# A graph layer on one core: adjacency moved against stationary features, instead of features moved against stationary adjacency

## The reference

```
h = maximum(layernorm(x), 0)
deg = sum(adj, axis=1) + 1e-5
out = (adj / deg) @ h @ W_neigh.T + b_neigh + h @ W_self.T + b_self
result = x + relu(out)
```

## Time and profile before

| | |
|---|---|
| median of three runs | 439.43 us |
| profiled execution, span from first to last instruction | 437.5 us (no other time is given for it) |
| TensorE busy | 423.0 us |
| VectorE busy | 210.6 us |
| ScalarE busy | 194.6 us |
| GpSimd busy | 57.0 us |
| first matmul (a transpose) / first main product | 8.18 us / 65.42 us |

### The profile page before, as it was taken

The page is one execution under the profiler, slowest core; times in us unless marked ns, Lnnn a source line. Parts: engine busy times, 40 slices in busy tenths (PEclk is TensorE's granted clock), DMA queues, the critical chain, the costliest instruction groups (busy, mean ns, idle before and its releaser), DMA issues.

```text
span 437.5 us, 9014 instructions
## 1 busy us (share of the span) xinstructions
PE 423.0 (97%) x3328; PEld 413.1 (94%) x3328; DVE 210.6 (48%) x263; ACT 194.6 (44%) x245; POOL 57.0 (13%) x76
## 2 busy tenths in 40 slices
PE   0899999999999999999999999999999999999996
PEld 0788889999999999999999999999999999999996
DVE  3667556334454336444544345435444454436344
ACT  3688765332534343433443353435343534343420
POOL 3465641000002000200002000200020002000200
PEclk9999999999999999999999999999999999999999
DMA  7900007555565656564667455755665465656511
GB/s 195 412 40 2 1 10 266 179 177 187 151 231 189 203 172 204 192 224 143 211 192 234 149 193 191 240 189 152 196 231 192 144 213 202 208 157 220 171 75 48
DMA packets 21291, 76.43 MB, mean 175 GB/s; under 512 B 2336, under 2 KB 3232, under 8 KB 21024
## 3 DMA queue, kind: packets, MB, share of 16 engines
q1 hardware_dynamic: 20272, 72.62, 50.7%
q0 software_dynamic: 1008, 3.67, 2.4%
HBM read 72.09 MB, written 4.19 MB: 174 GB/s over the span
## 4 chain that ended last, share of the span: by engine, by line
PE 96%; DMA 1%; POOL 0%; DVE 0%; SPq 0%; ACT 0%; issue 0%
PE banks L517 28%; PE banks L518 28%; PE banks L519 28%; PE banks L472 11%; PE banks L459 2%; DMA x_sb<-x_in 1%; ACT h_sb L219 0%; POOL rstd L177 0%; POOL rstd L180 0%; SPq L143 0%; SPq L144 0%; DVE self_sb L443 0%; DVE stats L317 0%; DVE x_sb L446 0%; SPq L128 0%
## 5 line engine op out<-in xcount | busy, mean ns | idle before, releaser
L518 PE MATMUL banks<-g_sb,adj_hi 128*128 (+1 forms) x1024 | 289.3, 283 | 0.0
L519 PE MATMUL banks<-g_sb,adj_lo 128*128 (+1 forms) x1024 | 289.3, 282 | 0.0
L517 PE MATMUL banks<-g_sb,adj_hi 128*128 (+1 forms) x1024 | 289.3, 282 | 0.0
L347 DVE TENSOR_TENSOR adj_lo<-adj_raw,adj_hi 128x1024 fp32r<-128x1024 f32 x128 | 159.1, 1253 | 191.6 <-ACT adj_hi L242 183.6
L242 ACT ACTIVATE adj_hi<-adj_raw 128x1024 fp32r<-128x1024 f32 x128 | 134.6, 1061 | 194.4 <-PE banks L519 194.2
L519 PEld LDWEIGHTS banks<-g_sb,adj_lo 128*128 128x128 f32 x1024 | 194.2, 190 | 0.0
L517 PEld LDWEIGHTS banks<-g_sb,adj_hi 128*128 128x128 f32 x1024 | 193.5, 189 | 0.0
L518 PEld LDWEIGHTS banks<-g_sb,adj_hi 128*128 128x128 f32 x1024 | 193.2, 189 | 0.0
L204 POOL TENSOR_TENSOR x_sb<-x_sb,self_sb 128x1024 f32<-128x1024 f32 x7 | 17.4, 2484 | 324.8 <-ACT self_sb L288 324.8
L472 PE MATMUL banks<-w_hi,adj_hi 128*128 128x512 f32 x64 | 27.3, 426 | 0.0
L472 PE MATMUL banks<-w_hi,adj_lo 128*128 128x512 f32 x64 | 25.9, 404 | 0.0
(11 more groups left out here) (30 smaller groups left out, 90.3 us busy)
## 6 DMA issues: line engine op xcount, KB each, us to landing
adj_raw<-adj_in SPq DMA_DIRECT2D x128, 512.0 KB, 3.4
rows_out<-x_sb POOLq DMA_DIRECT2D x7, 512.0 KB, 3.2
x_sb<-x_in SPq DMA_DIRECT2D x1, 2048.0 KB, 14.9
x_sb<-x_in SPq DMA_DIRECT2D x1, 1024.0 KB, 10.5
x_sb<-x_in SPq DMA_DIRECT2D x2, 256.0 KB, 4.0
x_sb<-x_in SPq DMA_DIRECT2D x1, 512.0 KB, 6.1
rows_out<-x_sb SPq DMA_DIRECT2D x1, 384.0 KB, 2.3
w_raw<-w_neigh SPq DMA_DIRECT2D x1, 256.0 KB, 3.6
```

Source lines behind the costliest of these rows:

```text
L347: nc.vector.tensor_tensor(adj_lo[:, r, :, :], adj_raw[:, r, :, :], adj_hi[:, r, :, :].bitcast(F32), ALU.subtract).then_inc(s_lo, 1)
L517: nc.tensor.matmul(bank[:, 0:GW], hi, g_hi, start=start, stop=False)
L518: nc.tensor.matmul(bank[:, 0:F], hi, g_lo, start=False, stop=False)
L519: product = nc.tensor.matmul(bank[:, 0:GW], lo, g_hi, start=False, stop=stop)
```

## The change

The order of the two products is turned round: (adj h) W in place of adj (h W). The high and low part of h (128 x 128 pieces) are now the stationary operand, and 512 columns of adjacency (512 output rows) move past them, so that a block's sums come out transposed, features on partitions, in two banks. Each block's sums are then split (`product_high`, `product_low`) and multiplied by W_neigh (`weigh`); the transposes of h and its product with W_self (`turn`, `own_product`) are spread over the main loop, which starts with the first unit. The first two blocks' units alternate, so that 32 units go with the 32 tiles of h. Degrees are no longer a column of the product: each raw unit is added to a running sum, on VectorE for the units that `on_vector` names and on GpSimd for the rest; the totals are joined, multiplied by a matrix of ones, and the diagonal is picked out (`degrees`). A slot of the ring is loaded anew only when its unit has been added too. Stores of all blocks go through SP's queue.

```diff
+def on_vector(s):
+    if s < 32:
+        return s in (14, 15, 18, 19, 22, 23, 26, 27)
+    if s < 48:
+        return s % 16 in (3, 9, 15)
+    return s % 16 in (2, 5, 8, 11, 15)
...
+    order = [(s % 2, s // 2) for s in range(2 * U)] + [(s // U, s % U) for s in range(2 * U, S)]
+    turn_at = [32, 39, 46] + [16 * q + 8 for q in range(3, Q)]
+    weigh_at = [36, 43, 52] + [16 * (q + 1) + 2 for q in range(3, Q)]
...
+            def load_unit(s):
+                q, u = order[s]
+                if s >= RING:
+                    old = s - RING
+                    sp.wait_ge(s_hi, old + 1)
+                    sp.wait_ge(s_lo, old + 1)
+                    if on_vector(old):
+                        sp.wait_ge(s_addv, added(old, True))
+                    else:
+                        sp.wait_ge(s_addg, added(old, False))
+                sp.dma_start(adj_raw[:, s % RING, :, :], adj[q, u, :, :, :]).then_inc(s_raw[s % RING], 16)
...
         @block.gpsimd
+            def add_unit(s):
+                q, _ = order[s]
+                total = sum_g[:, q % 2, :]
+                pool.wait_ge(s_raw[s % RING], 16 * (s // RING + 1))
+                if s == first_of(q, False):
+                    if q >= 2:
+                        pool.wait_ge(s_sums, q - 1)
+                    nc.gpsimd.tensor_tensor(total, adj_raw[:, s % RING, 0, :], adj_raw[:, s % RING, 1, :], ALU.add) \
+                      .then_inc(s_addg, 2)
+                else:
+                    pool.wait_ge(s_addg, added(s, False) - 2)
+                    nc.gpsimd.tensor_tensor(total, total, adj_raw[:, s % RING, 0, :], ALU.add).then_inc(s_addg, 1)
+                    pool.wait_ge(s_addg, added(s, False) - 1)
+                    nc.gpsimd.tensor_tensor(total, total, adj_raw[:, s % RING, 1, :], ALU.add).then_inc(s_addg, 1)
...
+            for s in range(S):
+                if not on_vector(s):
+                    add_unit(s)
+                if s >= 2 and s <= 26 and (s - 2) % 4 == 0:
+                    norm((s - 2) // 4 + 2)
+                for q in range(Q):
+                    if s == last_unit[q] + 1 or s == last_unit[q] == S - 1:
+                        join_sums(q)
+                    if s == turn_at[q] + 7:
+                        add_bias(q)
+                    if s == weigh_at[q] + 7:
+                        add_x(q)
...
         @block.scalar
+            for s in range(S):
+                split_unit(s)
+                if s % 2 == 0 and s // 2 + 1 < T // 2:
+                    make_h(s // 2 + 1)
+                if s % 2 == 1 and s // 2 + 1 < T // 2:
+                    split_h(s // 2 + 1)
...
         @block.vector
+            for s in range(2, S):
+                if s % 2 == 0 and s < T:
+                    split_h(s // 2)
+                split_unit(s)
+                if on_vector(s):
+                    add_unit(s)
...
+            def degrees(q):
+                dve.wait_ge(s_spread, q + 1)
+                nc.vector.tensor_tensor(picked[:, :, :], banks[:, SPREAD, :].rearrange("p (b i) -> p b i", b=UI),
+                                        ident[:, :].rearrange("p (a i) -> p a i", a=1).broadcast_to([P, UI, P]),
+                                        ALU.mult).then_inc(s_picked, 1)
+                dve.wait_ge(s_picked, q + 1)
+                nc.vector.tensor_reduce(deg[:, 0, :], picked[:, :, :], AX.X, ALU.add).then_inc(s_deg, 1)
...
         @block.tensor
+            def add_unit(s):
+                q, u = order[s]
+                r = s % RING
...
+                pe.wait_ge(s_lo, s + 1)
+                for k in range(KC):
+                    bank = banks[:, MAIN[q % 2][k], :]
+                    feats = slice(k * P, (k + 1) * P)
+                    for a in range(UJ):
+                        j = UJ * u + a
+                        first, last = j == 0, j == T - 1
+                        nc.tensor.matmul(bank, h_hi[:, j, feats], adj_hi[:, r, a, :], start=first, stop=False)
+                        nc.tensor.matmul(bank, h_lo[:, j, feats], adj_hi[:, r, a, :], start=False, stop=False)
+                        done = nc.tensor.matmul(bank, h_hi[:, j, feats], adj_lo[:, r, a, :], start=False, stop=last)
...
+            for s in range(S):
+                add_unit(s)
+                for q in range(Q):
+                    if s == turn_at[q]:
+                        turn(q)
+                    if s == turn_at[q] + 2:
+                        own_product(q)
+                    if s == weigh_at[q] - 1:
+                        spread_degrees(q)
+                    if s == weigh_at[q]:
+                        weigh(q)
+            spread_degrees(Q - 1)
+            weigh(Q - 1)
```

More of the change, by code:

```diff
@@ L54, in gnn_layer @@
         x_sb = sb("x_sb", [P, T, F])
[L55 to L59, removed]
+        h_hi = sb("h_hi", [P, T, F], F32R)
+        h_lo = sb("h_lo", [P, T, F], F32R)
+        adj_raw = sb("adj_raw", [P, RING, UJ, R])
+        adj_hi = sb("adj_hi", [P, RING, UJ, R], F32R)
+        adj_lo = sb("adj_lo", [P, RING, UJ, R], F32R)
+        h_row = sb("h_row", [P, 2, 2, F])
         w_raw = sb("w_raw", [P, KC, 2, F])
@@ L62, in gnn_layer @@
         w_lo = sb("w_lo", [P, KC, 2, F], F32R)
[L63 to L67, removed]
+        p_hi = sb("p_hi", [P, KC, R], F32R)
+        p_lo = sb("p_lo", [P, KC, R], F32R)
+        ht_hi = sb("ht_hi", [P, KC, R], F32R)
+        ht_lo = sb("ht_lo", [P, KC, R], F32R)
+        own = sb("own", [P, UI, F])
+        sum_v = sb("sum_v", [P, 2, R])
+        sum_g = sb("sum_g", [P, 2, R])
+        sums = sb("sums", [P, R])
+        sums_hi = sb("sums_hi", [P, R], F32R)
+        sums_lo = sb("sums_lo", [P, R], F32R)
+        picked = sb("picked", [P, UI, P])
+        ones = sb("ones", [P, P], F32R)
         ident = sb("ident", [P, P])
@@ new lines, in store_rows @@
+            def store_rows(q):
+                rows = slice(q * UI, (q + 1) * UI)
+                sp.wait_ge(s_final, q + 1)
+                sp.dma_start(out[:, rows, :], x_sb[:, rows, :]).then_inc(s_out, 16)
+            load_x(0)
+            load_unit(0)
+            load_unit(1)
+            load_x(1)
+            load_unit(2)
+            load_x(2)
+            load_unit(3)
+            load_x(3)
+            load_unit(4)
+            load_unit(5)
+            load_x(4)
+            load_unit(6)
@@ L152, in _ @@
[L152 to L158, removed]
+            for s in range(9, S):
+                load_unit(s)
+                for q in range(Q - 1):
+                    if s == weigh_at[q] + 12:
+                        store_rows(q)
@@ L162, in _, with add_x @@
+            def add_x(q):
+                rows = slice(q * UI, (q + 1) * UI)
+                pool.wait_ge(s_relu, q + 1)
+                nc.gpsimd.tensor_tensor(x_sb[:, rows, :], x_sb[:, rows, :], own[:, :, :], ALU.add).then_inc(s_final, 1)
             nc.gpsimd.memset(ident[:, :], 0.0).then_inc(s_zero, 1)
+            for n, value in enumerate((LN_EPS, -0.5, -1.0)):
+                nc.gpsimd.memset(consts[:, n, :], value).then_inc(s_consts, 1)
+            pool.wait_ge(s_consts, 3)
+            norm(0)
@@ L165, in _ @@
                                     base=0, pattern=[[-1, P]], channel_multiplier=1).then_inc(s_ident, 1)
[L166 to L198, removed]
@@ L201, in _ @@
[L201 to L208, removed]
+            nc.gpsimd.memset(ones[:, :].bitcast(F32), 1.0).then_inc(s_ones, 1)
@@ new lines, in _ @@
+            norm(1)
+            for s in range(S):
[10 more added lines that the diff above has]
+                        add_x(q)
@@ L210, in _ @@
         @block.scalar
         def _(act):
[L212 to L234, removed]
-                nc.scalar.activation(g_sb[:, tiles, 0:F], small[r % 2][:, :, 0:F], ACT.Copy)
-                nc.scalar.activation(self_sb[:, tiles, :], small[r % 2][:, :, F:2 * F], ACT.Copy).then_inc(s_ghi, 1)
@@ new lines, in join_rows @@
+            def join_rows(q):
+                dve.wait_ge(s_weighed, 2 * q + 2)
+                dve.wait_ge(s_ownb, q + 1)
+                dve.wait_ge(s_rdeg, q + 1)
+                for t in range(UI):
+                    last = nc.vector.scalar_tensor_tensor(
+                        out=own[:, t, :], in0=banks[:, SMALL[t // 2], (t % 2) * F:(t % 2 + 1) * F],
+                        scalar=deg[:, 2, t:t + 1], in1=own[:, t, :], op0=ALU.mult, op1=ALU.add)
+                last.then_inc(s_joined, 1)
@@ new lines, in _ @@
+            statistics(1)
+            means(1)
+            split_unit(1)
+            dve.wait_ge(s_x[2], 16)
+            statistics(2)
+            means(2)
+            for s in range(2, S):
[4 more added lines that the diff above has]
+                    add_unit(s)
+                if s % 4 == 1 and (s - 1) // 4 + 2 < len(groups):
+                    g = (s - 1) // 4 + 2
+                    dve.wait_ge(s_x[g // 2 + 1], 16)
+                    statistics(g)
+                    means(g)
+                if s == 21:
```

(59 more changed lines are left out.)

514 lines of the change are left out of this document (233 added, 281 removed).

## The result

The changed kernel takes 506.13 us (median of four, 503.49 to 508.36) against 439.16: ratio 1.1524, 95% interval 1.1483 to 1.1566. It is slower, as forecast, and inside the range; the forecast was 479. Its page: span, busy time by engine, and the granted clock in 40 slices.

The account below looks back on a forecast made before the run. TensorE bounded the kernel before; after the change, VectorE and GpSimd excluding each other in SBUF would. Sums ending at 130, 191 and 467 us plus a tail of 10.4 gave 478 of span, so 479 us; range 452 to 512.

Parts of the forecast that it names:

- TensorE's account: TensorE's products over the whole changed kernel: 420 us becomes 410, a gain of some 10 us on the bound engine.
- rival 2: Whole kernel: TensorE stays the bound and GpSimd's adds slip into VectorE's free times; 434 to 438 us, chance 0.12.
- The shared resource: VectorE instructions with two SBUF inputs and GpSimd's adds exclude each other: 1.08 us per 1024-column subtraction, 1.20 per add.
- first two stretches: Units 0 to 31, sum 117 us, until 130; units 32 to 47, sum 61 us, until 191.
- the third sum: Units 48 to 127: adds, joins, biases, residuals and subtractions sum to 276 us, until 467; TensorE needs 260.
- what hides the rest: Whole kernel: ScalarE, loads, stores and other waits are covered; ScalarE's 2.0 us a unit against 2.77 in the first 32.
- The tail: From the joined totals to the end, with no large product left to hide anything: 10.4 us.
- The forecast's own band: Time of the whole kernel if the forecast holds: 465 to 495 us, chance 0.52.
- rival 3: TensorE's lower clock level on top, products at 0.40 us in the first 32 units; 495 to 530 us, chance 0.18.
- Rival 1: Only the first 32 units are bound by the shared resource, TensorE afterwards; 461 us in all, chance 0.18.
- Most of the loss before 135 us: Sign that the forecast is right: most of the loss falls early in the kernel, before 135 us.
- The other observations named beforehand: Signs: GpSimd above 60% busy, adds beyond 1.3 us, adj_lo 1.6 to 2.4, TensorE some 86%, gaps released by adj_lo.

## Why the prediction was right, and where its size was off

- TensorE's account held: 410 us of products forecast, 411.5 busy without adds; 52 us a block (260 over five) against 50.7; the time without a price for the adds 434 to 438 (rival 2) against 434.86. What rival 2 lacked was its condition, two engines that do not exclude each other.
- The shared resource held as a mechanism (fills against adds) and as a price: 2.23 us for an add and a subtraction that alternate, first two stretches ending within some 1 us of the forecast. Counted from the rows, at least one of the two engines ran an instruction with two inputs in SBUF for 110.1, 61.2 and 275.3 us of the three stretches, where the sums are 117, 61 and 276. So the end of the first stretch is in part luck: the prices came out 7 us too high, and for 6.7 us neither engine ran one.
- The step that failed is the third sum, 276 us for units 48 to 127, and the paragraph on what hides the rest. It took the resource as never idle, and from 192.07 to 489.19 neither engine used it for 21.8 us. I had looked for waits of the loads, stores and norms, and not at the product with W_self, which stands in TensorE's order before the next unit and waits for a VectorE instruction that is itself queued behind held-up ones. GpSimd's last add ended at 477.8, 11 us late. It was not the last step of the sum either: the last unit's add is on VectorE, behind the same wait once more, so the join began only 10 us later and ended at 489.2. The tail, 10.4 forecast with no large product left, took 14.5 from there: in TensorE's order the products of two units, 5.5 us, still stood before the spreading of the degrees.
- That 506 lies inside the range is in part luck. The forecast's own band was 465 to 495; the range reached to 512 for a dearer add and for the slow level (rival 3), not for a wait in order. Of the wait the slow level was a part: 24 products at 0.21 in place of 0.12 make 2.6 us (2.87 to 5.49) in each block where it came.
- Rival 1 (no loss after unit 32) is refuted: 40 of the 71 us lie behind the first product with W_self. "Most of the loss before 135 us" was therefore wrong. Rival 3 named the slow level for the first 32 units. Its sign came there too, some 30 products before 130 us at 0.43 from start to start, as at 38 us, after gaps (granted clock 0.93 from 13 to 129.85); the stretch still ended as forecast. Most of it came in the steady blocks, 24 products at a time, after the wait.

```profile
38.15 0.63 PE L534 MATMUL banks<-adj_hi,h_hi 128*128 128x512 f32 x1
38.57 0.63 PE L535 MATMUL banks<-adj_hi,h_lo 128*128 128x512 f32 x1
39.00 0.63 PE L536 MATMUL banks<-adj_lo,h_hi 128*128 128x512 f32 x1
```

- The other observations named beforehand came: GpSimd 78% busy with its adds at 1.8 us on average, adj_lo at 2.2 in the middle, TensorE 86%, gaps ended by adj_lo.

## What to carry to other kernels

Before work is put on an engine that looks idle, look for places where it already met the busy one: ten lengthened instructions were enough here to price 176 new ones. Add the exclusive times of both engines as if they were one, stage by stage, and then walk each engine's order once more for instructions that wait behind a lengthened one; here that second step was worth 18 us (506.1 against 488.4 with the transposes earlier). And price the gain on the bound engine first: at 4 us of 439 it could pay for almost nothing.

## What was not expected of the hardware

A VectorE tensor_scalar on 128 x 4 elements, SBUF to SBUF with one input, is held up by GpSimd's adds too; by line (ns), in the changed kernel and without adds:

```profile
L450 DVE TENSOR_SCALAR deg<-deg x8: 170/1198/2191, 158.6 to 497.6; 128x4 f32<-128x4 f32 x8
```

```profile
L440 DVE TENSOR_SCALAR deg<-deg x8: 170/170/171, 127.3 to 426.7; 128x4 f32<-128x4 f32 x8
```

The reduction ahead of it (686 to 689 ns) and the reciprocal behind it (177 to 179) kept their times. With long fills in place of the adds it took 170 in the middle and 509 at most. Why this one is held was not tried. And products of 512 columns with a new stationary operand each kept to 0.227 to 0.230 us from start to start at the full clock, as in the earlier trace rows, only some 4% less per column than those of 256 to 258.
